# An attention and FFN kernel: the half-group stage reordered on four engines

## The reference, cut to what matters

```
h = einsum('bct,bcd->bdt', x, W1[condition])         # mixes the 32 tokens of a sequence
q, k, v = h @ wq, h @ wk, h @ wv                     # 4096, 1024, 1024 columns
q, k = rope(q), rope(k)                              # q*cos + rotate_half(q)*sin
scores = mask(q @ k.T / sqrt(128))                   # causal, 32 x 32 per sequence and head
x = x + (softmax(scores) @ v).reshape(...) @ wo      # 4096 -> 512
y = einsum('bct,bcd->bdt', x, W2[condition])
x = x + requantised_fp8(fp8(y) @ fp8(qweight).T * scales + bias)
```

## Time and profile before

| | us |
|---|---|
| median of three runs (737.14 to 743.44) | 740.24 |
| the profiled execution, its own time | 742.31 |
| span of the profiled execution | 740.5 |
| TensorE busy | 587.3 (79% of the span) |
| VectorE busy | 433.7 (59%) |
| GpSimd busy | 319.0 (43%) |
| ScalarE busy | 250.3 (34%) |
| HBM traffic over the span | 47 GB/s on average |

### The profile page before, as it was taken

The page is one execution under the profiler, slowest core; times in us unless marked ns, Lnnn a source line. Parts: engine busy times, 40 slices in busy tenths (PEclk is TensorE's granted clock), DMA queues, the critical chain, the costliest instruction groups (busy, mean ns, idle before and its releaser), DMA issues.

```text
span 740.5 us, 9212 instructions
## 1 busy us (share of the span) xinstructions
PE 587.3 (79%) x3150; PEld 465.9 (63%) x3150; DVE 433.7 (59%) x660; ACT 250.3 (34%) x477; POOL 319.0 (43%) x310
## 2 busy tenths in 40 slices
PE   8988985928993899668993899289948896798992
PEld 6866863827873687547772777268736775586840
DVE  5365768635566257724772467446652686367597
ACT  3331434340426033511442052404260335042253
POOL 2074886391267408470739043922664063230001
PEclk9999988768897879868995899788987898799997
DMA  7152120103010301030011201030102001200003
GB/s 257 57 185 86 57 86 0 43 2 113 1 42 1 114 0 42 0 113 0 0 42 43 70 0 42 0 113 0 42 0 71 15 1 60 72 15 1 1 0 113
DMA packets 32644, 35.27 MB, mean 48 GB/s; under 512 B 2251, under 2 KB 22859, under 8 KB 32620
## 3 DMA queue, kind: packets, MB, share of 16 engines
q1 hardware_dynamic: 32620, 34.96, 14.7%
HBM read 28.66 MB, written 6.29 MB: 47 GB/s over the span
## 4 chain that ended last, share of the span: by engine, by line
issue 37%; PE 29%; POOL 25%; DVE 6%; DMA 2%; ACT 1%; POOLq 1%; SPq 0%; DVEq 0%; ACTq 0%
POOL wq_lo L371 9%; POOL q_rot L385 7%; PE bank L724 6%; PE bank L725 5%; PE bank L726 5%; POOL wo_lo L380 4%; PE bank L784 3%; POOL k_rot L385 1%; DVE q_swap L1041 1%; DMA values<-v_st 1%; PE bank L696 1%; PE bank L667 1%; POOL w_sum L364 1%; PE bank L698 1%; PE bank L697 1%
## 5 line engine op out<-in xcount | busy, mean ns | idle before, releaser
L385 POOL TENSOR_TENSOR q_rot<-q_rot,q_swap 128x512 f32<-128x512 f32 x64 | 85.6, 1338 | 285.9 <-DVE q_swap L1041 285.9
L724 PE MATMUL bank<-wo_hi,o_hi 128*128 128x512 f32 x256 | 111.7, 436 | 103.7 <-POOL wo_lo L380 90.9
L1089 DVE TENSOR_TENSOR xacc<-xacc,bank 128x512 f32<-128x512 f32 x64 | 43.3, 677 | 149.4 <-PE bank L726 149.4
L724 PEld LDWEIGHTS bank<-wo_hi,o_hi 128*128 128x128 f32 x256 | 52.6, 205 | 122.9 <-issue 73.6
L531 ACT ACTIVATE o_hi<-bank 128x512 fp32r<-128x512 f32 x64 | 36.0, 598 | 233.9 <-PE bank L784 233.9
L725 PE MATMUL bank<-wo_lo,o_hi 128*128 128x512 f32 x256 | 107.4, 420 | 0.0
L726 PE MATMUL bank<-wo_hi,o_lo 128*128 128x512 f32 x256 | 107.1, 418 | 0.0
L514 ACT ACTIVATE q_swap<-bank 64x512 f32<-64x512 f32 x80 | 47.6, 596 | 108.7 <-DVE bank L1021 54.9
L784 PE MATMUL bank<-p_tr,v_st 32*128 32x128 f32 x512 | 57.6, 336 | 23.1 <-DVE s_nat L1047 11.6
L1041 DVE TENSOR_TENSOR q_swap<-q_swap,cst 128x512 f32<-128x512 f32 x80 | 72.4, 905 | 0.0
L784 PEld LDWEIGHTS bank<-p_tr,v_st 32*128 32x128 f32 x512 | 53.9, 232 | 29.2 <-issue 29.2
(11 more groups left out here) (161 smaller groups left out, 1095.1 us busy)
## 6 DMA issues: line engine op xcount, KB each, us to landing
raw_q<-in_L_attn_wq SPq DMA_DIRECT2D x16, 512.0 KB, 3.9
raw_o<-in_L_attn_wo SPq DMA_DIRECT2D x8, 1024.0 KB, 6.5
v_st<-values SPq DMA_DIRECT2D x16, 256.0 KB, 4.6
xacc<-in_x SPq DMA_DIRECT2D x4, 512.0 KB, 7.2
raw_k<-in_L_attn_wk SPq DMA_DIRECT2D x8, 256.0 KB, 4.3
values<-v_st SPq DMA_DIRECT2D x8, 256.0 KB, 2.0
out<-xacc SPq DMA_DIRECT2D x8, 256.0 KB, 2.0
raw_o<-in_L_attn_wv SPq DMA_DIRECT2D x1, 1024.0 KB, 8.0
```

The source lines that it names most:

```text
L385: pool.tensor_tensor(item_out(h, k), item_out(h, k), q_swap[(h + k) % 2][:], ALU.add).then_inc(rope_done, 1)
L724: pe.matmul(dst, l_hi, r_hi, start=(i == 0), stop=False)
L1089: dve.tensor_tensor(xacc[:, tile, :], xacc[:, tile, :], w_ps[j % 2][:], ALU.add).then_inc(acc_done, 1)
```

## The change

It changes the order of the steps in a half on GpSimd, ScalarE and VectorE, and the order of the 16 matmuls of `attend` on TensorE. No operation is added or removed.

- **GpSimd**: in h = 1 the four `wo_low` come before the `rope_add`s and no longer after them; `q_low` 0 to 3 also come before all `rope_add`s.
- **ScalarE**: `wo_high` comes before `exponent`; `q_high` 0 to 3 come before `swap(0)`; `q_high` 4, 5 and 6 follow `swap` 1, 2 and 3.
- **VectorE**: softmax step 3 comes after block sum 2 and step 4 after block sum 3; `accumulate` 0 comes between `rope(2)` and `rope(3)`, step 5 between `rope(3)` and `rope(4)`; `turn_scores` of group g moves from the start of half (g+1, 0) to the end of half (g, 1), ahead of the last `accumulate`.
- **TensorE**: `attend` loops over j outside and over the row tile b inside, so that matmuls that follow each other use different row tiles. The four increments of `pv_mm` now all come with the last four matmuls.

```diff
--- before.py
+++ after.py
@@ -401,21 +401,14 @@
                 more = not (isinstance(g, int) and g == KV - 1 and h == 1)
                 if more:
                     sum_weights(*follow)
-                rope_add(g, h, 0)
-                rope_add(g, h, 1)
-                if more:
-                    q_low(*follow, 0)
-                    q_low(*follow, 1)
-                rope_add(g, h, 2)
-                if more:
-                    q_low(*follow, 2)
-                rope_add(g, h, 3)
-                if more:
-                    q_low(*follow, 3)
-                rope_add(g, h, 4)
                 if split_wo is not None:
                     for head in range(REP):
                         wo_low(split_wo, head, wo_lo)
+                if more:
+                    for i in range(4):
+                        q_low(*follow, i)
+                for k in range(5):
+                    rope_add(g, h, k)
                 if more:
                     for i in range(4, PRODUCTS):
                         q_low(*follow, i)
@@ -547,27 +540,26 @@
                 if last is not None:
                     o_high(*last, 2)
                     o_high(*last, 3)
+                if split_wo is not None:
+                    wo_high(split_wo, wo_hi)
                 if soft is not None:
                     exponent(*soft)
+                if more:
+                    for i in range(4):
+                        q_high(*follow, i)
                 swap(g, h, 0)
                 swap(g, h, 1)
                 if more:
-                    q_high(*follow, 0)
-                    q_high(*follow, 1)
+                    q_high(*follow, 4)
                 swap(g, h, 2)
                 if more:
-                    q_high(*follow, 2)
+                    q_high(*follow, 5)
                 swap(g, h, 3)
                 if more:
-                    q_high(*follow, 3)
+                    q_high(*follow, 6)
                 swap(g, h, 4)
-                if split_wo is not None:
-                    wo_high(split_wo, wo_hi)
-                if more:
-                    for i in range(4, PRODUCTS):
-                        q_high(*follow, i)
-                    if h == 1:
-                        k_high(g + 1)
+                if more and h == 1:
+                    k_high(g + 1)
 
             half(0, 0)
             half(0, 1)
@@ -778,12 +770,13 @@
                 u = 2 * g + r
                 pe.wait_ge(dma_vst[r], 16 * (g + 1))
                 pe.wait_ge(soft_step, SOFT_STEPS * (u + 1))
-                for b in range(BPT):
-                    own = slice(T * b, T * (b + 1))
-                    for j in range(TPU):
+                for j in range(TPU):
+                    for b in range(BPT):
+                        own = slice(T * b, T * (b + 1))
                         mm = pe.matmul(ps[b][:, j * P:(j + 1) * P], v_st[r][own, j, :], p_tr[own, j * REP:(j + 1) * REP, :],
                                        start=True, stop=True)
-                    mm.then_inc(pv_mm, 1)
+                        if j == TPU - 1:
+                            mm.then_inc(pv_mm, 1)
 
             def project_out(g, r, j, left=(o_hi, o_lo), weights=(wo_hi, wo_lo)):
                 n = TPU * (2 * g + r) + j
@@ -1007,7 +1000,7 @@
                 else:
                     t_low(i - 2 * TPU)
 
-            def winograd(g, h, step):
+            def block_sum(g, h, step):
 
                 n = 2 * g + h
                 dve.wait_ge(prod_mm, PRODUCTS * n + SUM_PRODUCT[step])
@@ -1090,40 +1083,45 @@
 
             def half(g, h, last=None, weights=None, fill=()):
 
-                if weights is not None:
-                    if h == 0:
-                        turn_scores(g - 1, 0)
-                        turn_scores(g - 1, 1)
-                    for step in range(3):
-                        soft(*weights, step)
+                def soft_part(*steps):
+                    if weights is not None:
+                        for step in steps:
+                            soft(*weights, step)
+
+                def add_out(j):
+                    if last is not None:
+                        accumulate(*last, j)
+
+                soft_part(0, 1, 2)
                 if last is not None:
                     for b in range(BPT):
                         o_low(*last, b)
-                for step in range(5):
-                    winograd(g, h, step)
+                block_sum(g, h, 0)
+                block_sum(g, h, 1)
+                block_sum(g, h, 2)
+                soft_part(3)
+                block_sum(g, h, 3)
+                soft_part(4)
+                block_sum(g, h, 4)
                 rope(g, h, 0)
-                winograd(g, h, 5)
+                block_sum(g, h, 5)
                 rope(g, h, 1)
-                winograd(g, h, 6)
+                block_sum(g, h, 6)
                 rope(g, h, 2)
+                add_out(0)
                 rope(g, h, 3)
+                soft_part(5)
                 rope(g, h, 4)
                 for i in fill:
                     v_copy(i)
-                if last is not None:
-                    accumulate(*last, 0)
-                if weights is not None:
-                    soft(*weights, 3)
-                    soft(*weights, 4)
-                if last is not None:
-                    accumulate(*last, 1)
-                if weights is not None:
-                    soft(*weights, 5)
-                    soft(*weights, 6)
-                if last is not None:
-                    accumulate(*last, 2)
-                    if not (isinstance(g, int) and 2 * g + h == 2 * KV - 1):
-                        accumulate(*last, 3)
+                add_out(1)
+                soft_part(6)
+                add_out(2)
+                if h == 1:
+                    turn_scores(g, 0)
+                    turn_scores(g, 1)
+                if not (isinstance(g, int) and 2 * g + h == 2 * KV - 1):
+                    add_out(3)
 
             dve.wait_ge(dma_const, 32)
             half(0, 0, fill=late[0:2])
@@ -1155,8 +1153,6 @@
                 dve.tensor_reduce(y_max[:, t:t + 1], y_t(t), AX_X, ALU.max,
                                   apply_absolute_value=True).then_inc(y_amax, 1)
 
-            turn_scores(KV - 1, 0)
-            turn_scores(KV - 1, 1)
             for b in range(BPT):
                 o_low(KV - 2, 1, b, o2_ps, o2_hi, o2_lo)
             accumulate(KV - 2, 0, 3)
```

## The result

The changed kernel takes 558.46 us (median of 4 runs, 555.35 to 560.26) against 739.94 us before: a ratio of 0.754 (95% interval 0.749 to 0.759), 24.6% less. Forecast were 570 us, 553 to 608. The profiled execution has a span of 557.7 us against 740.5, and its mean granted clock rose from 0.871 to 0.973.

What follows compares the result with a forecast made beforehand. TensorE, busy 79% of 740.5 us, was held back by waits (121.5 us) and low clock. Turns fall from 79.07 to 54.4 us, five saving 123.5; with the other stretches 171.1 off 742.3 gives 571, put at 570 us, range 553 to 608.

Steps and rivals of the forecast that it cites:

- The output weights first: In h = 1, wo_low starts 5.2 us after the attend and ends at 10.1; the 13.5 us wait before projections goes.
- What is late next: In h = 1 the rope_add chain runs from 13.9 to 23.8, giving a new 0.9 us wait before the scores.
- The scores turned first: turn_scores runs beside the last projection, so the 2.4 us wait and 3.1 us of low clock behind it go.
- accumulate(0) and the softmax steps: On VectorE accumulate(0) no longer waits for all five ropes: 2.0 us go; softmax steps 3 and 4 fall into gaps.
- The attend: On TensorE alternating row tiles shorten each attend from 2.8 to 1.4 us, saving 1.4 us, 16 times.
- What the short attend uncovers: In each half product 2 waits for o_low(0) on VectorE: 0.6 us, bounds 0 and 0.8.
- The start of half (1,1): It comes 3.2 us earlier: half (1,0)'s chain shrinks by 1.8, and two softmax steps (1.4) go into gaps.
- The tail: Behind the last half, three shorter attends save 4.2 us.
- row tiles that don't overlap: Rival on TensorE: attend stays at 2.8 us, giving 585 us; chance 0.12.
- The stretched rope chain: Rival: VectorE and GpSimd share a path, adding 5.5 us before the scores in six halves, 603 us; chance 0.20.
- The wait for `wo_low`: Rival: wo_high is held up, so wo_low and projection 0 follow, 7 x 12.6 us more, 658 us; chance 0.03.
- the slower clock: Rival on TensorE: denser work or reordered attends take the clock to 0.50 for good, 909 us; chance 0.03.

Runs made afterwards that it cites:

- e1: Kernel before with only wo_high ahead of exponent and the four wo_low ahead of the rope_adds in h = 1: 638.55 us (ratio 0.863).
- e8: e7 with, in addition, the four wo_low behind the five rope_adds and wo_high behind swap(4): 645.38 us (ratio 0.871).
- e2: Kernel before with only turn_scores moved to the end of half (g,1), ahead of the last accumulate: 705.58 us (ratio 0.952).
- e6: Changed kernel with turn_scores back at the start of h = 0: 573.43 us (ratio 0.775).
- e7: Changed kernel with softmax steps 3 to 6 and the accumulates at their places of before on VectorE, turn_scores staying early: 578.43 us (ratio 0.782).
- e9: Changed kernel with q_low and q_high 0 to 3 back among the rope_adds and swaps: 562.73 us (ratio 0.760).
- e11: e10 with, in the tail, the four o_low of unit (7,0) ahead of accumulate(6,1,3) on VectorE: 551.57 us (ratio 0.747).
- e5: Changed kernel with the attend's loops in their old order: 585.03 us (ratio 0.790).
- e3: Kernel before with only the attend's loops exchanged, so that row tiles alternate: 702.19 us (ratio 0.948).
- e10: Changed kernel with, in h = 1, only q_low(0) ahead of rope_add(0) and q_low 1 to 3 in the rope chain's gaps: 556.4 us (ratio 0.751).
- e12: Kernel before with 58 extra unused matmuls on TensorE ahead of the first projection in h = 1, filling the whole stand: 729.25 us (ratio 0.986).
- e4: Kernel before with 50 extra unused matmuls on TensorE ahead of the first projection in h = 1: 733.44 us (ratio 0.987).

## Why the prediction was right, step by step

The sum came to 171.1 us less, the spans show 182.8. By stretch, forecast and measured: five loop turns 123.5 and 129.8; start of half (1,1) 3.2 and 129.93 - 122.08 = 7.9; half (1,1) 20.3 and 20.7; half (7,0) 5.6 and 6.3; half (7,1) 14.3 and 15.0; tail 4.2 and 3.0. Five of the six gave more than forecast and only the tail less, so the total isn't right by errors that cancel.

- **The output weights first**: right in mechanism, place and size. e1 alone brings 101 of the 181 us, and e8 shows the stand come back.
- **What is late next**: right. The wait before the scores was put at 0.9 us and is 0.8, from a `rope_add` chain that starts at 13.7 and ends at 23.1.
- **The scores turned first**: right. Its 2.4 + 3.1 us a turn are e2's 34 us. In the changed kernel the same step is worth 15 (e6), because the clock doesn't fall behind each such stand.
- **accumulate(0) and the softmax steps**: right that the 2.0 us go; undone in e7, they bring 2.8 us a turn back, clock included.
- **The attend**: right that it overlaps, and too cautious: 1.10 us from its start to the first product (177.43 to 178.53), not 1.4. The estimate by "TensorE: Matmul & The Clock Gate" of the Trainium skill (Part 3, Measured speedup vs the span model) was 0.9 us; the trace lies between, and the measurement decides. From start to start an attend took 2.75 us before, so it saves 1.65 and not 1.4, which is 2.5 us over the ten attends of the loop.
- **What the short attend uncovers**: the term of 0.6 us a half was too large (its own numbers, 4.9 less 4.2, give 0.7). Measured are 0.15 us before product 2 (it starts at 181.54; at the 0.23 us between the starts before it, it was due at 181.39), and 0.15 to 0.25 in all on the products of a half. That is some 4 us over the ten halves; with the attend it makes up nearly all of the 6.3 us by which the loop beat the forecast. I had let two softmax steps be stretched beside GpSimd. Only one of them is in each half, step 2 here and step 0 in the next:

```profile
178.14 0.71 DVE L1050 TENSOR_TENSOR s_nat<-s_nat,cst 128x512 f32<-128x512 f32 x1
...
179.60 1.21 DVE L1054 TENSOR_TENSOR s_nat<-s_nat,s_max 128x512 f32<-128x512 f32 x1
...
206.21 1.13 DVE L1050 TENSOR_TENSOR s_nat<-s_nat,cst 128x512 f32<-128x512 f32 x1
```

- **The start of half (1,1)**: what the step named is right, 3.2 us forecast and 3.4 measured, as the wait before that attend goes from 9.5 to 6.1 us. But the step left out half (0,1), which gives 4.4 more. There, too, the chain ends last and is shorter, so the scores wait 1.0 us and not 2.8, and with the shorter stand the clock stays at 1.00: scores and products behind it take 12.54 us (100.52 to 113.06), and took 15.29 at a mean of 0.78 (102.21 to 117.50). e9 puts 4 us of it down to `q_low` ahead of the ropes.
- **The tail**: its three attends gained 5.0 us, more than the 4.2, but the 36 projection matmuls behind the stand of 3.2 us take 11.1 us, and took 9.7. By the spread shown under e11 these 1.4 us are the clock's chance in one execution more than an effect of the change. Another 0.5 us is lost in the 48 projection matmuls after the first attend (11.87 us against 11.40), half of it a wait.
- **The rivals**: row tiles that don't overlap are ruled out by the 1.17 us. The stretched rope chain is not seen: 9.4 us from first to last `rope_add`, and the five sine products of that half took 0.7 to 1.0 us, none 1.8. The wait for `wo_low` did not stay, and the clock rose. The argument against the slower clock, that it is at 0.50 only behind a stand of over 2 us, is too strong: e5 shows it without one.

How much of the gain a part has depends on what else is there. Alone, weights, turned scores and attend bring 101 + 34 + 37 = 172 us. Taken out of the changed kernel one by one, turned scores and attend cost 15 and 27, and the weights cost 67 on top of e7. For the turned scores the traces show that the difference is clock. The six stands are 13.6 us long in both kernels. In the kernel before, attend and products behind them took up to 17.17 us, where e2 has 12.49 each time, 21.8 us more in all; in e6 the same places cost 3.9.

```profile
180.98:198.15 17.17, 17.17 (x74) 14.50 (x75) 8.88 (x15) 5.66 (x10) 0.00 (x0) 0.70 0.01 1
```

Why the clock stays low for longer behind the same stand in the kernel before is open.

## What to carry to other kernels

Look on each in-order engine for work that waits for nothing new but stands behind a chain, and put it where its inputs are ready; then follow the chain that was pushed back to its next waiter, and work out its end, since that is the new wait. A stand of the matmul engine of over 2 us cost its own length and, behind it, between nothing and 4.7 us of low clock here (17.17 against 12.49 us). Closing one stand among several brought more than closing the last (34 us in e2, 15 in e6). Put a sum that waits for the matmul engine where what is queued behind it can wait too.

## What the runs showed of the hardware

- Matmuls of 32 rows that change the row tile each time take 37 ns each in the changed kernel (1.17 us for 32 records at clock 1.00; 65 ns at 0.50 in e3), against 88 ns when eight records in a row use one tile (2.82 us for 32).
- A stand of 2.3 us was followed by the low clock in some halves and not in others of the same execution (e6: three of six). Behind the same stand of 3.2 us in the tail, the same 36 matmuls took 8.4, 9.7, 10.0 or 11.1 us (e6, before, e10, changed).
- In the changed kernel the loop's stretches of 52 us between two waits of 0.8 us stayed at 1.00. In e5 the clock fell once, 34 us after the last stand, one of 1.05 us. It also did once in e12 (products of 11.33 us from 517.48) and twice in e4, some 9 us behind a wait of 1.5 to 1.6 us. Each time an attend in the old order had just run; whether that has to do with it is not shown.
- Filling 11.5 of 13.8 us of a stand with matmuls left the clock falling behind it in three of seven halves (e4); when all of it was filled, the 36 projection matmuls took 8.5 to 8.6 us in all seven (e12).
